# Where the rotary attention's first q tiles are computed: two of them inside the expert layer's last steps, eight inside the first lap

## The reference, cut to what matters

```
x = x + tanh(g_ffn[0]) * L0_ffn(layernorm(x))        # 14 weight tiles of experts, two halves of the tokens
x = x + tanh(g_xattn[1]) * L1_xattn(layernorm(x), ctx_512)
L1_xattn:  16 heads, taken here as 8 pairs
  q_big  = rope((hidden @ Wq.T) @ w_kc_q)            # q: product, then times cos, times sin, and the sum
  q_r    = q_big @ W_qr
  scores = q_r . k_r ; attn = softmax(scores) ; ctx = attn @ kv ; out = ctx @ w_kc_kv @ Wo.T
```

## Time and profile before

| | us |
|---|---|
| median of three runs | 545.96 |
| the profiled execution | 546.06 |
| its span | 543.9 |
| PE busy (share of the span) | 496.7 (91%) |
| DVE busy | 415.2 (76%) |
| ACT busy | 308.6 (57%) |
| POOL busy | 280.3 (52%) |
| mean granted clock of PE, full speed being 1 | 0.959 |

### The profile page before, as it was taken

The page is one execution under the profiler, slowest core; times in us unless marked ns, Lnnn a source line. Parts: engine busy times, 40 slices in busy tenths (PEclk is TensorE's granted clock), DMA queues, the critical chain, the costliest instruction groups (busy, mean ns, idle before and its releaser), DMA issues.

```text
span 543.9 us, 9155 instructions
## 1 busy us (share of the span) xinstructions
PE 496.7 (91%) x2775; PEld 382.8 (70%) x2775; DVE 415.2 (76%) x1060; ACT 308.6 (57%) x789; POOL 280.3 (52%) x291
## 2 busy tenths in 40 slices
PE   6886999998997997789999999999998977999996
PEld 3664678876876885557777777777776756778874
DVE  4998599988477658888999999999997874644322
ACT  3744554433644643267877777787777772155541
POOL 0042446765433842658777778786661016436560
PEclk9969799999999999879999999999999996999998
DMA  7659313322422319944727180807004602334426
GB/s 255 206 187 302 135 50 93 87 62 59 145 85 62 88 39 227 180 109 96 150 55 170 36 192 11 193 10 166 1 2 186 290 5 84 107 105 127 127 64 231
DMA packets 40281, 65.02 MB, mean 120 GB/s; under 512 B 4324, under 2 KB 30638, under 8 KB 39985
## 3 DMA queue, kind: packets, MB, share of 16 engines
q1 hardware_dynamic: 37984, 60.31, 39.4%
q0 software_dynamic: 2256, 4.21, 2.4%
HBM read 38.48 MB, written 27.99 MB: 122 GB/s over the span
## 4 chain that ended last, share of the span: by engine, by line
PE 65%; DVE 21%; ACT 4%; issue 3%; DMA 3%; POOL 1%; another core or an unknown queue 1%; SPq 1%; POOLq 0%; DVEq 0%
PE bank L1588 10%; PE bank L802 9%; PE bank L1643 5%; PE bank L1632 5%; PE bank L1662 5%; PE bank L1006 5%; PE bank L837 4%; PE bank L1605 3%; PE bank L1609 3%; PE bank L1622 3%; PE bank L1623 2%; PE bank L1022 2%; DVE xn L359 2%; DVE hid L758 2%; DVE silu L756 2%
## 5 line engine op out<-in xcount | busy, mean ns | idle before, releaser
L1423 POOL TENSOR_TENSOR qr<-qr 128x512 f32<-128x512 f32 x48 | 61.6, 1283 | 15.9 <-DVE qr L2078 15.9
L2078 DVE TENSOR_TENSOR qr<-bank,sinq 64x512 f32<-64x512 f32 x96 | 66.1, 689 | 2.2
L1815 ACT ACTIVATE silu<-bank,negm 128x256 f32<-128x256 f32 x128 | 59.2, 470 | 5.9 <-DVE negm L2092 5.9
L719 POOL TENSOR_TENSOR ffn_w_l<-ffn_raw,ffn_w_h 128x512 fp32r<-128x512 f32 x30 | 39.4, 1315 | 35.3 <-ACT ffn_w_h L731 35.2
L1428 POOL TENSOR_TENSOR hid<-silu,rden 128x256 f32<-128x256 f32 x55 | 33.7, 613 | 36.4 <-DVE rden L2097 36.4
L743 ACT ACTIVATE hid_h<-hid 128x512 fp32r<-128x512 f32 x28 | 17.7, 631 | 55.5 <-DVE hid L758 49.2
L2092 DVE TENSOR_REDUCE negm<-bank 128x2 f32<-128x512 f32 x64 | 44.2, 691 | 6.4 <-PE bank L1623 3.7
L1822 ACT ACTIVATE hid<-silu,rden 128x256 f32<-128x256 f32 x55 | 27.9, 507 | 34.2 <-DVE rden L2097 34.2
L961 POOL DMA_INDIRECT y_rows<-moe_y,route_rows x31 | 30.1, 971 | 30.7 <-issue 16.8
L802 PE MATMUL bank<-xT_h,ffn_w_h 128*128 128x512 f32 x120 | 41.4, 428 | 2.9 <-DVE xT_l L416 2.9
L1828 ACT ACTIVATE probsT<-bank 128x512 f32<-128x512 f32 x64 | 37.9, 592 | 10.1 <-PE bank L1632 9.7
(11 more groups left out here) (255 smaller groups left out, 1395.2 us busy)
## 6 DMA issues: line engine op xcount, KB each, us to landing
xn_slots<-blank SPq DMA_DIRECT2D x8, 2056.0 KB, 12.5
ffn_raw<-in_w_ffn SPq DMA_DIRECT2D x30, 256.0 KB, 2.7
pair_w<-in_pair_w SPq DMA_DIRECT2D x8, 768.0 KB, 5.2
moe_w<-in_w_moe SPq DMA_DIRECT2D x1, 6144.0 KB, 17.9
moe_x<-xn_slots SPq DMA_DIRECT2D x31, 128.5 KB
ffn_raw<-in_w_ffn SPq DMA_DIRECT2D x30, 128.0 KB, 2.4
folds<-att_w_raw SPq DMA_DIRECT2D x6, 640.0 KB, 7.5
att_w_raw<-folds SPq DMA_DIRECT2D x6, 384.0 KB, 12.1
```

The lines of the kernel that those rows point to most:

```text
L719: nc.gpsimd.tensor_tensor(wt_l[b][:, 0:GU], raw[b][:, 0:GU], wt_h[b][:, 0:GU], ALU.subtract).then_inc(self.wgl, 1)
L1423: nc.gpsimd.tensor_tensor(qr[n][:, 0, :], qr[n][:, 0, :], qr[n][:, 1, :], ALU.add).then_inc(s_turned, 1)
L1815: last = nc.scalar.activation(ex[u % 2][:, h, :], bank[4 + u % 2][:, h * S:(h + 1) * S], ACT.Exp, bias=negm[:, u % 2, h:h + 1], accum_out= ...
L2078: last = nc.vector.tensor_tensor(by_sin[other, :, :], q2[hs, :, :], sinq[hs, j:j + 1, :].broadcast_to([C, 2, S]), ALU.mult)
```

## The change

It moves q tiles and their `cos_sin`, and lets the maxima of the first lap begin earlier in DVE's list.

- PE: tile (0, 0) in step 25, (0, 1) in step 26 (was: only (0, 0), in step 26). After the expert layer (0, 2), (1, 0), (1, 1), the transposes, (0, 3), the rope step. Then the lap, with (0, 4), (0, 5), (1, 2), (1, 3), (1, 4), (1, 5) in slots 0 to 5. (1, 2) leaves `FIRST_BANKS`, and so takes the general wait. The rope step of pair 0's second half waits for 12 on `s_cs`; the wait for 10 ahead of the laps is gone.
- DVE: `cos_sin` (0, 0) ahead of step 26, (0, 1) ahead of the sum, (0, 2) after the norm's apply, (0, 3) after `xT_l`, then `q_low`, and in slots 0 to 7 of the lap (0, 4), (0, 5), (1, 0), (1, 1), (1, 2), (1, 3), (1, 4), (1, 5).
- POOL: three turned tiles ahead of the second expert layer's low parts, one behind them, the others one slot behind their `cos_sin`; the last one at the end of slot 7.
- ACT: `q_high` ahead of the splits of the second expert layer's first tile. The first part of pair 2's weights is split in slot 2, not 1.
- SP: the two clearing transfers go behind the laps' loop.

```diff
+        def q_order(i, n):
+            early = ((0, 0), (0, 1), (0, 2), (1, 0), (1, 1), (0, 3), (0, 4), (0, 5))
+            return early.index((i, n)) + 1 if isinstance(i, int) and (i, n) in early else i * 6 + (n + 1)
...
-        Q_AT, FIRST_Q_AT = {0: 1, 1: 2, 3: 3, 4: 4, 5: 5}, {1: 2, 3: 3, 4: 4, 5: 5}
-        COS_AT, FIRST_COS_AT = {0: 0, 1: 1, 2: 2, 4: 3, 5: 4, 6: 5}, {0: 0, 1: 1, 2: 2, 4: 3, 5: 4, 6: 5}
+        Q_AT, COS_AT = {0: 1, 1: 2, 3: 3, 4: 4, 5: 5}, {0: 0, 1: 1, 2: 2, 4: 3, 5: 4, 6: 5}
+        FIRST_Q_AT = {0: ((0, 4),), 1: ((0, 5),), 2: ((1, 2),), 3: ((1, 3),), 4: ((1, 4),), 5: ((1, 5),)}
+        FIRST_COS_AT = {0: ((0, 4),), 1: ((0, 5),), 2: ((1, 0),), 3: ((1, 1),), 4: ((1, 2),), 5: ((1, 3),),
+                        6: ((1, 4),), 7: ((1, 5),)}
-        FIRST_BANKS = {(0, 0): 6, (0, 1): 2, (0, 2): 0, (0, 3): 7, (0, 4): 6, (0, 5): 7, (1, 0): 3, (1, 1): 1, (1, 2): 0}
+        FIRST_BANKS = {(0, 0): 6, (0, 1): 7, (0, 2): 0, (0, 3): 6, (0, 4): 7, (0, 5): 2, (1, 0): 3, (1, 1): 1}
+        FIRST_W_AT = {2: 0, 4: 1}
...
                 sp.wait_ge(s_zz, 3)
-                for i in range(NPAIR - 2, CLEARS):
-                    clear_slots(i)
                 with sp.Fori(0, (NPAIR - 2) // 2) as ii:
...
+                for i in range(NPAIR - 2, CLEARS):
+                    clear_slots(i)
                 sp.wait_ge(s_rp, NPAIR * 2 * JT)
...
-                    elif (i, n) == (0, 5):
-                        pe.wait_ge(s_cs, 8)
...
+                    if isinstance(i, int) and (i, c) == (0, 1):
+                        pe.wait_ge(s_cs, 2 * 2 * JT)
...
-                              N0 + 2: lambda: comb_pe(route[0][1], pe), 2 * N0 - 2: first_q_step},
+                              N0 + 2: lambda: comb_pe(route[0][1], pe), **{2 * N0 - 3 + n: partial(first_q_step, n) for n in range(2)}},
...
-                for i, n in ((0, 1), (0, 2), (1, 0), (1, 1)):
+                for i, n in ((0, 2), (1, 0), (1, 1)):
                     q_step(i, i, n)
                 n_att[1].pe_transpose(pe)
                 n_att[1].pe_whole(pe)
                 q_step(0, 0, 3)
-                q_step(0, 0, 4)
                 rope_step(0, 0, 1, 0)
-                q_step(0, 0, 5)
-                pe.wait_ge(s_cs, 10)
...
+                q_high(0, 0, 0)
                 split_first_tile()
-                q_high(0, 0, 0)
...
-                                    2 * N0 - 5: lambda: n_att[0].low(dve)}, topk_round, first_cos_sin)
+                                    2 * N0 - 5: lambda: n_att[0].low(dve), 2 * N0 - 2: lambda: first_cos_sin(0)},
+                                topk_round, lambda: first_cos_sin(1))
...
-                cos_sin(0, 1)
+                first_cos_sin(2)
                 n_att[1].low(dve)
-                cos_sin(0, 2)
                 cos_sin(0, 3)
-                cos_sin(0, 4)
                 q_low(0, 0, 0)
-                cos_sin(0, 5)
```

More of the change, by code:

```diff
@@ L8 @@
 from contextlib import ExitStack
+from functools import partial
 import numpy as np
@@ L1250, in shared, with tiles, q_tiles, cos_tiles @@
                 return self.q
[L1252 to L1256, removed]
+            def tiles(self, n, first, at):
+                if self.first:
+                    return [(i, i, tile) for i, tile in first.get(n, ())]
+                return [(self.i, self.b, at[n])] if self.q and n in at else []
+            def q_tiles(self, n):
+                return self.tiles(n, FIRST_Q_AT, Q_AT)
+            def cos_tiles(self, n):
+                return self.tiles(n, FIRST_COS_AT, COS_AT)
             def rope(self, n):
@@ L1278, in weights @@
                     return None
+                if self.first:
+                    return FIRST_W_AT.get(n)
                 return (LATE_PARTS if isinstance(self.i, int) and self.i == NPAIR - 2 else W_AT).get(n)
@@ L1450, in slot @@
                         normalise(before[0], before[2])
-                    tile = lap.cos_tile(n - 1)
-                    if tile is not None:
-                        turned(lap.i, tile)
+                    for i, _, tile in lap.cos_tiles(n - 1):
+                        turned(i, tile)
                     if n == 0 and lap.softmax and not lateness(lap.i - 1):
@@ L1461, in slot @@
                         low_part(lap.i + 1, 1 - lap.b, m)
+                    if n == NU - 1:
+                        for i, _, tile in lap.cos_tiles(n):
+                            turned(i, tile)
                 pool.wait_ge(ffn0.hl, 1)
@@ L1465, in _ @@
                                       2 * N0 - 5: lambda: low_part(1, 1, 0), 2 * N0 - 4: lambda: low_part(1, 1, 1)})
-                turned(0, 0)
-                turned(0, 1)
+                for n in range(JT):
+                    turned(0, n)
                 for st in (ffn1_first, ffn1_second):
                     ffn1.low_gateup(pool, st)
-                for n in range(2, 2 * JT):
-                    turned(0, n)
+                turned(0, JT)
                 pool.sem_inc(s_parts, 2)
@@ L1676, in slot @@
                         values(*half)
-                    m = lap.q_tile(n)
-                    if m is not None:
-                        q_step(lap.i, lap.b, m)
+                    for tile in lap.q_tiles(n):
+                        q_step(*tile)
                     if n == NEXT_Q_AT and lap.more:
@@ L1683, in slot, with first_q_step @@
                         project(*batch)
-                def first_q_step():
-                    n_att[0].pe_whole(pe)
-                    q_step(0, 0, 0)
+                def first_q_step(n):
+                    if n == 0:
+                        n_att[0].pe_whole(pe)
+                    q_step(0, 0, n)
                 ffn0.prog_pe(pe, {1: lambda: rows_pe(route[0][0], pe),
@@ L2062, in second_rows, with first_cos_sin @@
                     dve.wait_ge(route[0][1].rowc, 2)
-                def first_cos_sin():
-                    dve.wait_ge(s_trig, 32)
-                    cos_sin(0, 0)
+                def first_cos_sin(n):
+                    if n == 0:
+                        dve.wait_ge(s_trig, 32)
+                    cos_sin(0, n)
                 def cos_sin(i, n):
@@ L2069, in cos_sin @@
                         dve.wait_ge(s_rp, i * (2 * JT) + JT * (n // JT) - JT)
-                    dve.wait_ge(s_q, i * 6 + (n + 1 + 2 * (n >= JT and isinstance(i, int) and i == 0)))
+                    dve.wait_ge(s_q, q_order(i, n))
                     q2 = bank[bank_of(i, n)][:].rearrange("p (b s) -> p b s", b=2)
@@ L2119, in slot @@
                     unit, before = lap.unit(n, 0), lap.unit(n, 1)
-                    half, m, done = lap.q_low(n), lap.cos_tile(n), lap.batches(n, ADDED)
+                    half, done = lap.q_low(n), lap.batches(n, ADDED)
                     heads = () if lap.shared() else (0, 1)
@@ L2142, in slot @@
                         normalise(before[0], before[2], heads)
-                    if m is not None:
-                        cos_sin(lap.i, m)
+                    for i, _, tile in lap.cos_tiles(n):
+                        cos_sin(i, tile)
                 for r in range(AHEAD):
```

## The result

| | before | changed |
|---|---|---|
| median of 4 runs, us | 546.25 (545.31 to 547.03) | 560.46 (558.20 to 563.17) |
| profiled execution, us | 546.06 | 561.09 |
| its span, us | 543.9 | 559.2 |
| mean granted clock | 0.959 | 0.951 |

The ratio is 1.025 [1.0221, 1.0278]: slower by 14.2 us in the medians and by 15.0 in the two profiled executions. The forecast was 556.0, in a range of 550.0 to 561.5 with 0.89 on slower. The ratios in this document leave out three executions in a slow state (625.75 and 551.23 us of the kernel before, 1198.36 us with its clearings moved), which the medians count and which shift a median by at most 0.4.

What follows compares the result with a forecast made beforehand. PE sets the settled laps, with DVE 1.0 us behind, so a first-lap delay is not won back. 546.06 + 7.2 (second lap's later begin) + 2.8 (low clock) = 556.1, written 556.0; range 550.0 to 561.5.

Steps and rivals of the forecast that it cites:

- step 6: PE's clock to the second lap's begin: low-level matmuls behind idle time cost 0 to 8.3 us; a third, 2.8, taken.
- rival B: The low clock throughout: +7.2 + 8.3 us, 561.6 in all; chance 0.14.
- Step 1: Expert layer's end: chain to the norm starts 1.4 us later, a `cos_sin` hidden in DVE's idle time; sum at 209.65.
- Step 2: Lap's begin: the rope step follows tile (0, 3) at once; first maxima at 226.6, 2.55 us earlier.
- Rival E: Lap's begin: low clock on tile (0, 3) and rope step, first maxima not earlier; 555.8 us; inside the forecast's 0.66.
- Step 3: Slots 0 to 2: a `cos_sin` in each, 2.93 us on DVE; second half's `q_high` until 237.3, 1.5 still won.
- Step 4: Slots 3 to 5: q tile, scores, maxima and `cos_sin` form three rings of 4.92 us, DVE idle 2.0 each; 6.0 us.
- C: First lap's rings: one instead of three, since PE runs late and `q_low` covers the others; 550.6 us; chance 0.09.
- D: The first lap absorbs two tiles, banks free when PE comes; mark moves -0.25, 545.8 us; chance 0.11.
- Step 5: Slots 6 and 7: second lap's first `cos_sin`, the mark, at 262.1 instead of 254.90, +7.2 us.
- Step 7: Behind the loop: three clearings follow each other from about 377, over by 415, ahead of the load at about 424; no cost.

Runs made afterwards that it cites:

- with fills, the begin filled: Changed kernel with last three q tiles a slot later, plus matmuls of zeros ahead of transposes, tile (0, 3) and first scores: 551.02 us, ratio 1.0096.
- the version without a ring, q tiles later: Changed kernel with q tiles (1, 3), (1, 4), (1, 5) in slots 4, 5, 6 instead of 3, 4, 5: 551.85 us, ratio 1.0103.
- the lap alone: Changed kernel with the early tiles undone, on DVE too; the lap keeps its eight `cos_sin` and its order: 555.53 us, ratio 1.0221.
- PE filled in the rings: Changed kernel with ten matmuls of zeros on PE ahead of the waiting q tile in slots 3 to 5: 558.84 us, ratio 1.0249.
- clearings back: Changed kernel with the two clearing transfers back ahead of the laps: 560.27 us, ratio 1.0267.
- the early tile alone: Kernel before with only (0, 0) and (0, 1) in the expert layer's last two steps, and the lap of before: 547.64 us, ratio 1.0049.

## Why the prediction was right, and where it was off

The direction, the place and the mechanism were right; the size was too small by 5.0 in the profiled execution, and the term is that of step 6. That the median still lies in the range is partly luck: by 1.0 us, with one of the four runs (563.17) outside, and that end of the range came from rival B, not from the forecast. Times below are less 0.63, by which the changed kernel began its stretch later.

- **Step 1** held: a `cos_sin` at 202.49 between `hid_l` and silu, with 0.58 of idle time left. The sum is at 209.94 instead of 209.65: `hid_l` took 1.00 instead of the 0.69 of the earlier trace rows, beside a `turned` on POOL.
- **Step 2** was right at the full clock (226.22 with fills) and wrong as it happened: first maxima at 228.75, 2.15 late. Rival E's mechanism: tile (0, 3) took 2.86 instead of 2.14, and the rope step and the first scores behind it were partly or wholly low too. The lap won 0.4 at its first maxima, not 2.55.
- **Step 3**: the second half's `q_low` at 240.50 instead of 237.3: 3.2 late. With the begin filled it came as forecast, so the 3.2 are the clock.
- **Step 4** held: the three rings stand in slots 3 to 5, released as named. Ring and idle time at the full clock are 4.93 and 2.03, to 0.01 and 0.03, and their price over the version without a ring is 6.0, as forecast. The sentence that would have refuted the prediction, L1588 not waiting in these slots, did not come true. Rivals C and D fell: three rings, not one, and the last two tiles were not absorbed.
- **Step 5** held: from the maxima of unit 6 to the mark 8.51, forecast 8.6.
- **Step 6 failed in size.** 2.8 was taken; it came to 7.7: 3.2 at the begin and 4.5 in the rings. 7.2 + 7.7 = 14.9, the measured stretch. The two parts come from two kernels; none was run with the begin and the rings filled at once. My bound was 8.3, and its parts came out differently. The rings had 4.3. The rope step of slot 6, with 1.6, cost nothing: it ran at the full level (262.21, 1.08). The begin had 2.4, all of it for rope steps, and cost more, because tile (0, 3) (2.86 instead of 2.14), the first scores (1.03 instead of 0.48) and tile (0, 4) (2.22 instead of 1.50) were low too; the bound had no term for these. The choice of a third rested on the earlier trace rows, a window with 2.75 of 5.00 busy at 0.95. The window right behind it, at 0.50, was as near, and I gave it the smaller weight without a reason. I had no row of a PE that waits several times in a row for 2 us and keeps its clock.
- **Step 7** held: the clearings follow each other from 382.24, and the next load is at 429.56.

Rival B, the low clock throughout, gave 561.6; measured 561.1 in the profiled execution and 560.46 in the median. It had 0.14 and deserved more. The Trainium skill, "TensorE: Matmul & The Clock Gate", section "HAM oscillation — how this bites in real kernels", which has each short burst between waits start at the low clock, was nearer to the changed kernel than my reading of one window. But the case told there has longer waits (about 3 to 5 us; here 1.95 to 2.97), and with the lap alone two of three rings ran at the full clock. The Trainium skill, "TensorE: Matmul & The Clock Gate", section "What's actually happening", says that the number of matmuls that run cold differs from run to run. That agrees: four kernels with the same order up to slot 3 (changed, PE filled in the rings, clearings back, q tiles later) came to the second half's `q_low` 39.25, 39.31, 39.84 and 41.15 after the stretch's start.

## What to carry to other kernels

When an operation that waits for another engine is moved, count for each slot what is queued behind it, and ask whether the engine that frees it needs that very work next: a freeing product in the same slot as the waiting tile makes a ring of both engines, and one slot of distance takes it away (10.5 us over three slots here). A stall on TensorE can be paid twice, once as idle time and once as matmuls at half speed behind it (6.0 and 4.5 us in these rings). Where several short stalls follow each other, compute both prices and don't rest on the cheaper: of the three kernels with this ring and no fills, two ran it low and one mostly full. And judge such an edit by a stretch between two fixed instructions as well as by the total, for the rest of the program moves by some us from run to run.

## What the chip showed that I had not expected

- Matmuls of zeros into a free bank kept the granted clock at 1.00 through waits in which it was 0.65 to 0.67 without them.
- DVE's `hid_l`, which reads two tiles of the on-chip memory, took 1.00 instead of 0.69 where it started beside POOL's `turned`. That one took 1.74 instead of 1.27; it had itself started beside DVE's `hid`, which kept its 0.92. Each time the later of the two was the longer. With the early tile alone `hid_l` and `turned` took 1.00 and 1.73. Timelines of the changed kernel:

```profile
205.90 0.92 DVE L759 TENSOR_TENSOR hid<-silu,rows 128x512 f32<-128x512 f32 x1
...
206.23 1.74 POOL L1439 TENSOR_TENSOR qr<-qr 128x512 f32<-128x512 f32 x1
```

  The Trainium skill, "Advanced Engine Details and Errata", section "GPSIMD Details", says that Pool shares a read and a write interface with DVE and conflicts with DVE instructions that have two SBUF inputs; the trace agrees.
- Two kernels with the same rings ran them at different clocks (19.32 and 15.59 us for three), so even a forecast with every wait named has some 4 us of spread from the clock.
